# A graph attention kernel whose first 56 steps take one row in fourteen from rows of x that were gathered early

## The reference, cut to what matters

```
def _gat_layer(h_in, W, a_s, a_d, b, src, dst, n):
    h = (h_in @ W).reshape(n, Hh, Cc)
    alpha_s = jnp.sum(h * a_s, axis=-1)
    alpha_d = jnp.sum(h * a_d, axis=-1)
    e = jax.nn.leaky_relu(alpha_s[src] + alpha_d[dst], 0.2)
    m = jax.lax.stop_gradient(jax.ops.segment_max(e, dst, num_segments=n))
    ex = jnp.exp(e - m[dst])
    alpha = ex / jax.ops.segment_sum(ex, dst, num_segments=n)[dst]
    out = jax.ops.segment_sum(h[src] * alpha[:, :, None], dst, num_segments=n)
    return out.reshape(n, Hh * Cc) + b
...
h = jnp.maximum(_layernorm(x, axis=-1), 0.0)
h = gelu(_gat_layer(h, W0, ...))      # layer 0
h = gelu(_gat_layer(h, W1, ...))      # layer 1
x = x + h
```

## Time and profile before

| | |
|---|---|
| median of 3 executions | 4951.69 us (4951.07 to 4952.96) |
| span of the profiled execution, first to last instruction | 4186.7 us |
| median less span | 765.0 us |
| first gather of layer 0 | at 160.65 us |
| last gather of layer 0 | at 2132.16 us |
| first gather of layer 1 | at 2175.73 us |

### The profile page before, as it was taken

One profiled execution on the slowest core, in us unless ns is written; L12 is line 12 of the kernel. 1 busy time (PEld: TensorE's weight loads), 2 busy tenths in 40 slices (PEclk: granted clock), 3 DMA queues, 4 the chain that ended last, 5 costly groups with the idle time before them and its releaser, 6 DMA issues.

```text
span 4186.7 us, 56110 instructions
## 1 busy us (share of the span) xinstructions
PE 2764.1 (66%) x9786; PEld 1887.3 (45%) x9786; DVE 3644.9 (87%) x13061; ACT 2255.3 (54%) x7170; POOL 3044.4 (73%) x3215
## 2 busy tenths in 40 slices
PE   7566676666676666667655666666666666666666
PEld 6344444444444444444433444444444444444444
DVE  6588888888888888888868999999999999999998
ACT  5355555555555555555544555555555555555555
POOL 4477777777777777777747777777777777777774
PEclk9777878777777777877777777777777777777777
DMA  7555555555555555555535555555555555555553
GB/s 227 169 148 152 152 151 153 152 152 152 152 152 151 150 150 152 152 150 153 150 104 148 158 158 158 160 159 159 159 159 159 158 159 159 159 159 156 159 157 103
DMA packets 326665, 645.47 MB, mean 154 GB/s; under 512 B 97682, under 2 KB 195386, under 8 KB 326634
## 3 DMA queue, kind: packets, MB, share of 16 engines
q0 software_dynamic: 152224, 429.04, 38.2%
q1 hardware_dynamic: 128664, 172.56, 13.4%
q10 hardware_dynamic: 45746, 43.56, 3.0%
HBM read 597.18 MB, written 47.71 MB: 154 GB/s over the span
## 4 chain that ended last, share of the span: by engine, by line
POOL 54%; issue 22%; PE 13%; DMA 7%; DVE 3%; POOLq 0%; SPq 0%; ACT 0%; ACTq 0%; DVEq 0%
POOL rows_all L512 53%; PE bank L1129 10%; DMA rows_all<-table,edge 5%; DMA edges<-rows_all 2%; PE bank L1137 1%; PE bank L1151 1%; DVE rows_all L890 1%; PE bank L1116 0%; DVE ahead L901 0%; DVE value L895 0%; DVE onehot L910 0%; DVE behind L903 0%; DMA before_i<-in_dst_dram 0%; PE bank L1117 0%; PE bank L1122 0%
## 5 line engine op out<-in xcount | busy, mean ns | idle before, releaser
L512 POOL DMA_INDIRECT rows_all<-table,edge x3136 | 2990.4, 954 | 1008.5 <-issue 978.7
L1129 PE MATMUL bank<-rows_all,onehot 128*128 128x264 f32 x6272 | 1871.6, 457 | 20.7 <-DVE rows_all L890 11.0
L1129 PEld LDWEIGHTS bank<-rows_all,onehot 128*128 128x128 f32 x6272 | 1383.7, 228 | 458.3 <-DVE rows_all L890 186.2
L587 ACT ACTIVATE rows_all<-rows_all 128x64 f32<-128x64 f32 x3584 | 878.3, 336 | 3.7
L1111 PE MATMUL bank<-onehotT,logit_p 128*128 128x448 bf16 x896 | 279.3, 448 | 769.9 <-DVE logit_p L881 769.9
L890 DVE TENSOR_TENSOR rows_all<-rows_all,bank 128x768 f32<-128x768 f32 (+1 forms) x672 | 658.6, 1036 | 0.0
L1111 PEld LDWEIGHTS bank<-onehotT,logit_p 128*128 128x128 bf16 x896 | 79.9, 110 | 925.1 <-DVE logit_p L881 861.9
L1116 PE MATMUL bank<-ident,ahead 128*4 128x128 f32 x224 | 83.6, 373 | 581.6 <-DVE behind L903 581.0
L910 DVE TENSOR_TENSOR onehot<-bank,dloc 128x1792 f32<-128x1792 f32 x224 | 453.4, 2024 | 7.7
L599 ACT ACTIVATE share<-node_d 128x8 f32<-128x8 f32 x224 | 46.8, 209 | 742.7 <-DVE node_d L959 742.7
L611 ACT ACTIVATE bank<-fall 128x56 f32<-128x56 f32 x224 | 49.5, 221 | 579.8 <-DVE fall L987 579.8
(11 more groups left out here) (173 smaller groups left out, 3694.2 us busy)
## 6 DMA issues: line engine op xcount, KB each, us to landing
dst_b<-dst_row SPq DMA_DIRECT2D x224, 448.0 KB, 4.1
rows_all<-table,edge POOLq DMA_INDIRECT x3136
self_row<-table SPq DMA_DIRECT2D x224, 132.0 KB
table<-row ACTq DMA_DIRECT2D x113, 132.0 KB
x_row<-in_x_dram SPq DMA_DIRECT2D x112, 128.0 KB, 2.5
out_dram<-y_out ACTq DMA_DIRECT2D x112, 128.0 KB
table<-row ACTq DMA_DIRECT2D x24, 528.0 KB, 4.3
xg<-in_x_dram SPq DMA_DIRECT2D x24, 512.0 KB, 3.8
```

The lines of the kernel that those rows point to most:

```text
L512: nc.gpsimd.indirect_dma_start(out=G[u][:, j, :], out_offset=None, in_=table[L][0:N, :], in_offset=bass.IndirectOffsetOnAxis(ap=index[:, j ...
L587: last = nc.scalar.activation(G4[t.u][:, j, h, 0:C], G4[t.u][:, j, h, 0:C], ACT.Copy, scale=G4[t.u][:, j, h, C:C + 1])
L1129: last = nc.tensor.matmul(bank[3 + t.half][:, 0:ROW], onehot[t.half][:, j, :], G[t.u][:, j, :], start=(j == 0), stop=(j == SLOTS - 1))
```

## The change

For the first 56 chunks the rows of one slot (the last, number 13) are no longer gathered from `table[0]`. Instead the rows of x for that slot are gathered into SBUF during the dense stage: POOL issues two such gathers after each of the 28 stores of the edge lists. DVE computes their means and variances (14 chunks per set, four sets; the first two sets between groups of the dense stage, the last two after it). In the first 56 steps of layer 0, ACT normalises the 128 rows (`early_norm`), PE transposes them (`early_transpose`) and multiplies them by the first layer's weights (`early_rows`), with an ACT copy in between (`early_copy`), and ACT moves the product into slot 13 of the step's buffer (`early_move`). POOL issues 13 gathers in these steps instead of 14.

The index list for the early gathers comes from the source indices, whose load moves ahead on SP. To make room for `early_x` (56 tiles of 128 rows), many buffers now share their space: those of the dense stage with those of the steps. So SP, ACT and DVE get waits for the end of the dense stage and its stores. The loop of layer 0 is split in a head (14 rounds) and a rest.

```
+    EARLY = 56
+    AHEAD = EARLY // NB
+    HEAD_SETS = 4
+    IN_SET = EARLY // HEAD_SETS
...
+        early_T = bank[7][:, 0:KC * P]
+        early_row = bank[7][:, 0:ROW]
...
-        xg = [sb(f"xg{b}", [P, GROUP, D]) for b in range(XB)]
+        xg = [groups_or_hots[:, b * GROUP * D:(b + 1) * GROUP * D].rearrange("p (t c) -> p t c", t=GROUP) for b in range(XB)]
...
@@ pipeline
+                if L == 0:
+                    run(0, -ROLES, counts, skip=ROLES, head=True, coming=True)
                 for j in range(ROLES - 1):
-                    run(0, j + 1 - ROLES, counts, skip=ROLES - 1 - j)
-                with eng.Fori(0, rounds_) as r:
+                    run(0, j + 1 - ROLES, counts, skip=ROLES - 1 - j, head=L == 0, coming=L == 0)
+                if L == 0:
+                    with eng.Fori(0, AHEAD - 2) as r:
+                        counts = {}
+                        for j in range(NB):
+                            run(r, j, counts, head=True, coming=True)
+                    counts = {}
+                    for j in range(NB):
+                        run(AHEAD - 2, j, counts, head=True, coming=j < NB - 1)
+                with eng.Fori(AHEAD - 1 if L == 0 else 0, rounds_) as r:
@@ SP
+            sp.dma_start(src_c[0:96, :], src[0:96 * CH].rearrange("(c e) -> c e", e=CH)).then_inc(first_src_landed, 16)
...
-            sp.dma_start(src_c[0:96, :], src[0:96 * CH].rearrange("(c e) -> c e", e=CH)).then_inc(src_landed, 16)
...
+            for k in range(2):
+                sp.wait_ge(hnT_done[k], GROUPS * GROUP // 2 + 1 + 1)
@@ POOL
             for n in range(PIECES):
                 piece = slice(n * PIECE, (n + 1) * PIECE)
                 pool.dma_start(to[0:CHUNKS, piece], whole[0:CHUNKS, piece]).then_inc(edges_stored, 16)
-
+                for c in range(n * EARLY // PIECES, (n + 1) * EARLY // PIECES):
+                    nc.gpsimd.indirect_dma_start(
+                        out=early_x[:, c, :], out_offset=None, in_=x[0:N, :],
+                        in_offset=bass.IndirectOffsetOnAxis(ap=early_i[:, c:c + 1], axis=0)).then_inc(early_landed[c // IN_SET], 16)
                 pool.wait_ge(edges_stored, 16 * (n + 1))
...
-                        for j in range(SLOTS):
+                        for j in range(slots):
...
+                if L == 0:
+                    with nc.gpsimd.Fori(0, AHEAD) as r:
+                        gather_round(r, {}, SLOTS - 1)
+                with nc.gpsimd.Fori(AHEAD if L == 0 else 0, rounds_ + 1) as r:
+                    gather_round(r, {}, SLOTS)
@@ ACT
+            def early_norm(e):
+                chunk = act.value_load(steps_i[0:1, T_CHUNK, bass.ds(e.k, 1)], min_val=0, max_val=EARLY - 1)
+                act.wait_ge(s["earlyT_done"], e.done(1))
+                nc.scalar.activation(early_h, early_x[:, bass.ds(chunk, 1), :].rearrange("p o c -> p (o c)"), ACT.Relu,
+                                     bias=early_shift[:, bass.ds(chunk, 1)], scale=early_rstd[:, bass.ds(chunk, 1)]).then_inc(s["early_normed"], 1)
+
+            def early_copy(e):
+                act.wait_ge(s["earlyT_done"], e.done(0))
+                act.wait_ge(s["early_row_done"], e.done(1))
+                nc.scalar.activation(early_hT[:], early_T.rearrange("c (k n) -> c k n", n=P), ACT.Copy).then_inc(s["earlyT_copied"], 1)
+
+            def early_move(e):
+                act.wait_ge(s["early_row_done"], e.done(0))
+                act.wait_ge(s["sum_done"], e.done(4))
+                nc.scalar.activation(G[e.u][:, SLOTS - 1, :], early_row, ACT.Identity).then_inc(s["early_row_moved"], 1)
...
@@ DVE
+            def early_stats_of(c0, c1):
+                dve.wait_ge(early_landed[c0 // IN_SET], 16 * IN_SET)
+                n = c1 - c0
+                for j in range(n):
+                    last = nc.vector.bn_stats(early_stats[:, j, :], early_x[:, c0 + j, :])
+                link(last)
+                for j in range(n):
+                    last = nc.vector.bn_aggr(early_mv[:, c0 + j, :], early_stats[:, j, :])
+                return last
...
+            link(early_stats_of(0, 3))
             fill_fields()
...
+            link(early_stats_of(2 * IN_SET, 3 * IN_SET))
+            early_stats_of(3 * IN_SET, EARLY).then_inc(early_scaled, 1)
...
             def take_values(t):
-                dve.wait_ge(s["landed"][t.u], t.landed(16 * SLOTS))
+                if t.head:
+                    dve.wait_ge(s["landed"][t.u], t.landed(16 * (SLOTS - 1)))
+                    dve.wait_ge(s["early_row_moved"], t.done(0))
...
@@ PE
+            def early_transpose(e, stored_):
+                pe.wait_ge(s["early_normed"], e.done(0))
+                pe.wait_ge(s["early_row_moved"], e.done(1))
+                if stored_:
+                    pe.wait_ge(s["row_copied"], stored_.done(0))
...
+            def early_rows(e):
+                pe.wait_ge(s["earlyT_copied"], e.done(0))
...
+                    if known_ and known_.head:
+                        pe.wait_ge(s["early_row_moved"], known_.done(0))
                     next_rows(stored_)
...
+                if coming:
+                    early_transpose(coming, stored_)
+                    early_rows(coming)
                 if known_:
                     logits_to_edges(known_)
```

More of the change, by code:

```diff
@@ L294, in pipeline, with run @@
             for L in range(2):
-                def run(r, first, counts, n=ROLES, skip=0):
-                    body(*[None if j < skip or j >= n else Step(eng, L, r, rounds_, first + j, counts) for j in range(ROLES)])
+                def run(r, first, counts, n=ROLES, skip=0, head=False, coming=False):
+                    steps_of = [None if j < skip or j >= n else Step(eng, L, r, rounds_, first + j, counts, head) for j in range(ROLES)]
+                    body(*steps_of, Step(eng, L, r, rounds_, first + ROLES, counts, True) if coming else None)
                 counts = {}
+                if L == 0:
+                    run(0, -ROLES, counts, skip=ROLES, head=True, coming=True)
                 for j in range(ROLES - 1):
-                    run(0, j + 1 - ROLES, counts, skip=ROLES - 1 - j)
-                with eng.Fori(0, rounds_) as r:
+                    run(0, j + 1 - ROLES, counts, skip=ROLES - 1 - j, head=L == 0, coming=L == 0)
[8 more added lines that the diff above has]
+                with eng.Fori(AHEAD - 1 if L == 0 else 0, rounds_) as r:
                     counts = {}
@@ L804, in _ @@
             count_up()
+            early_indices()
             LIST = TURNS - 4
-            with nc.vector.Fori(0, LIST) as i:
+            for j in range(XB):
+                between(Group(0, j), Group(0, j + 1))
+                if j == 1:
+                    early_list()
+            with nc.vector.Fori(1, LIST) as i:
                 for j in range(XB):
@@ L1153, in next_rows, with pe_body @@
                     last.then_inc(s["row_done"], 1)
-            def pe_body(stored_, finished, weighed, landed, known_):
+            def early_transpose(e, stored_):
[3 more added lines that the diff above has]
+                    pe.wait_ge(s["row_copied"], stored_.done(0))
+                for j in range(KC):
+                    last = nc.tensor.transpose(early_T[:, j * P:(j + 1) * P], early_h[:, j * P:(j + 1) * P], ident[:])
+                last.then_inc(s["earlyT_done"], 1)
+            def early_rows(e):
+                pe.wait_ge(s["earlyT_copied"], e.done(0))
+                for j in range(KC):
+                    last = nc.tensor.matmul(early_row, early_hT[:, j, :], w_ext[:, 0, j, :], start=(j == 0), stop=(j == KC - 1))
+                last.then_inc(s["early_row_done"], 1)
+            def pe_body(stored_, finished, weighed, landed, known_, coming):
                 if stored_:
```

120 lines of the change are left out of this document (91 added, 29 removed).

## The result

The change takes 4997.16 us (median of 4, 4982.2 to 5022.18) against 4951.88 us (4951.07 to 4952.96) before. The ratio is 1.0097 with a 95% interval of 1.007 to 1.0125. The forecast was 4918 us; the change is 45 us slower instead of 34 us faster.

A forecast was written before the change was run, and what follows sets the result against it. POOL's gathers were taken to bound each step, with DVE 1.4 us behind. Start +27 us and head -61 us made -34; span 4152.7 us plus 765.0 us outside the instructions gave 4918 us, range 4893 to 4962.

The forecast's parts named there:

- DVE's second semaphore: In the steps, DVE was to get only a second semaphore in a wait it already had; no cost was counted.
- Layer 1 ... do not change: Layer 1 and the second half of layer 0 were to keep their time; no term was counted for them.
- The base: Profiled span 4186.7 us, steps of 17.6 us, taken as typical; the 765.0 us up to the median kept as outside instructions.
- DVE's margin of 1.4 us: In layer 0 DVE was put 1.4 us per step behind POOL, the most that a step could gain.
- 16.5 us per step: Expected length of a head step with 13 gathers, down from 17.6 us.
- the drain's 16.1 us: Where layer 0 drains, two successive DVE products start 16.1 us apart, taken as DVE's step without waits.
- Removed gathers: Layer 0's head: 56 gathers fewer on POOL, 1.1 us per step, 61 us gained; ends 70 and 34 us.
- Edge lists and source load: At the start: early gathers lengthen POOL's chain of stores by 25 us, moved source-index load adds 2 us; +27 us.
- Rival 1: At the start: stores finish only with the gathers behind them, periods 6.1 us, chain +72 us, total 4965 us; chance 0.15.
- The 3.9 us: Edge-list stores: short periods become 3.9 instead of 3.3 us if a store cannot land before the gather ahead of it.
- Products on ACT and PE: Head steps: added ACT and PE work mostly hidden in their waits for DVE; up to 1 us per step if cover is gone.
- Rival 2: Head: late copy on ACT or PE's sums push DVE, step settles at 17.0 us, gain 34 us, 4945 us; chance 0.20.

The follow-up runs named there:

- b1: The kernel before, unchanged, profiled again beside its timed executions: 4949.97 us, ratio 0.9998, steps 21.06 us apart.
- b3: The change's dense part alone (early gathers, statistics, shared buffers, split loop), 14 gathers per step, no products: 4974.64 us, 1.0043 of the kernel before.
- b4: The change without products in the head, 13 gathers there, slot 13 zero, dense part kept: 4891.1 us, 0.9882 of the kernel before.
- e4: The change without DVE's second wait behind the head and with `early_copy` behind the `Gelu`, full products: 4908.79 us, 0.9908 of the kernel before.
- d: Runs on one slower chip: the change without head products, 4980.57 us; with products, `early_copy` behind the `Gelu` and no second DVE wait behind the head, 5042.76 us.
- e1: The change without products, but ACT does its three head instructions on SBUF data and PE nothing: 4896.15 us, 0.9883 of the kernel before.
- e2: The change without products, but PE transposes and multiplies fixed operands in the head and ACT does nothing: 4886.64 us, 0.9875 of the kernel before.
- e3: The change with both ACT's and PE's head work but no wait between the two for it: 4903.29 us, 0.9910 of the kernel before.
- c1: The change without DVE's second wait behind the head, copy still ahead of the `Gelu`: 5044.12 us, 1.0017 of the kernel before.
- c3: The change without DVE's second wait behind the head and with `early_copy` behind the `Gelu`: 5032.0 us, 0.9987 of the kernel before.
- c4: The change, unchanged, measured again on a slower chip: 5114.15 us, 1.0126 of the kernel before.
- f1: The change, unchanged, measured once more on another slower chip: 5093.2 us, 1.012 of the kernel before.
- f2: The change without DVE's second wait behind the head, copy ahead of the `Gelu`, measured once more: 5057.45 us, 1.0036 of the kernel before.
- f: Side-by-side runs on one slower chip: the change, 5093.2 us, and the change without DVE's second wait behind the head, 5057.45 us.
- c: Four runs on one slower chip, among them the change, 5114.15 us, and the change without DVE's second wait behind the head, 5044.12 us.
- c2: The kernel before with one already met wait more per step on DVE: 5058.01 us, 1.0023 of the kernel before.
- d4: The kernel before with SP's load of `self_row` made once instead of per step: 5012.49 us, 0.9953 of the kernel before.
- b2: The kernel before with 13 gathers in all 224 steps, slot 13 zero: 4727.92 us, 0.955 of the kernel before.

## Why the prediction was wrong

Two steps of the prediction failed. The step that turned the sign is the term that it put at nothing: DVE's second semaphore, and with it "Layer 1 ... do not change". The other is its base, the profiled execution, which made all margins per step wrong but did not cost the gain.

In the profiled execution the change came out at +71.3 us where -34 were forecast, 105 us apart: layer 1 +84.5, the head +31 (-29.7 for -61), the start -9 (+18.3 for +27), the rest -2. Without layer 1's 84.5 us the change would have been 13 us shorter than the kernel before, even in this slowest of its executions.

**The base: that the profiled execution stands for the timed ones, and that the 765 us between span and median lie outside the instructions and stay.** All spans profiled later, of both kernels, end about 2 us below their own time. The 762 us are 3.4 us in each of 224 steps, in pauses as those of b1. So POOL's pace of 1.256 us per gather times 14 was not the whole step, and DVE's margin of 1.4 us, 16.5 us per step and the drain's 16.1 us described an execution that did not recur.

**Removed gathers: right in kind, sized too low.** Forecast 1.1 us per head step, -61 us. Measured without the products: 1.5 us per step (19.54 against 21.06), -83.5 us from b3 to b4.

**Edge lists and source load: close in sum, by luck in part.** The first gather came at 180.1 us, forecast 188: +19 for +27. Two terms were off in opposite directions. The stores' chain grew by 15.6 us, not 25, and the load of the source indices cost 4.5 us, not 2: the chain of waits of the change has it as

```profile
10.76 13.51 DMA before_i<-in_dst_dram
```

against the earlier trace rows. The stores stand 4.11 us apart (forecast 4.4), from 53.6 to 164.5 us. Waits for their landing, in one period of the middle and at the end, timeline of POOL:

```profile
80.87 0.58 POOL L529 DMA_DIRECT2D edges<-rows_all  x1 [2.08 <-DMA edges<-rows_all]
81.76 0.97 POOL L531 DMA_INDIRECT early_x<-in_x_dram,early_i  x1 [0.30 <-issue]
83.04 1.12 POOL L531 DMA_INDIRECT early_x<-in_x_dram,early_i  x1 [0.30 <-issue]
86.32 0.58 POOL L529 DMA_DIRECT2D edges<-rows_all  x1 [2.16 <-DMA edges<-rows_all]
...
161.44 0.58 POOL L529 DMA_DIRECT2D edges<-rows_all  x1
162.32 0.97 POOL L531 DMA_INDIRECT early_x<-in_x_dram,early_i  x1 [0.30 <-issue]
163.60 0.95 POOL L531 DMA_INDIRECT early_x<-in_x_dram,early_i  x1 [0.30 <-issue]
164.55 0.58 POOL L529 DMA_DIRECT2D edges<-rows_all  x1
```

Up to 149 us the periods lie between 3.1 and 6.4 us, 4.3 on average; the last six are 3.1 us, which is POOL's own work (3.32 in the prediction). Half of the stores wait for a landing at all, 25.6 us in 14 waits. (The row at 147.52 us in the earlier trace rows, which the prediction takes for the last of the 28 stores, is the first store behind them; the 28 periods are right.) Rival 1 wanted over 5.6 us on average; it did not happen, and the slower result is not its doing. The 3.9 us that the prediction worked out for the short periods from the Trainium skill's "DMA: Bandwidth & Descriptors" (section "Queues, rings and completion order") were not paid. That does not speak against the rule: the store at 161.44 had landed by 164.55, and the gather ahead of it, issued at 160.50, was due after the 3.77 us of the earlier trace rows at 164.3.

**Products on ACT and PE: put at nothing beyond the 16.5 us, and not free.** They cost 18 to 22 us on the chips that run the kernel before at 4950 us (e4) and 62 us on the chip of d. Each engine alone has room (e1, e2). The prediction followed the copy to ACT's `Gelu` and gave PE's wait of 3.64 us as cover, but it did not price the path of five handoffs in a row (normalise, transpose, copy, multiply, move), each behind other work in order. The profiled heads fit with that path as the cause (e4's is 24 us longer than b4's and 18 longer than e3's); the medians of e3 and e4 do not bear it out, so it stays an argument. Rival 2 named the effect; that its 34 us of gain lie near the 29.7 measured is chance, since it took them from a step of 17.0 us that did not exist. In the change itself the head is 25 us longer than in e4 (1150.7 against 1125.8), in profiled executions on two chips that run the kernel before alike; the copy ahead of the `Gelu` and the second wait are what differs. Whether either is the cause was not settled: c1 and c3 differ by 12 us, inside their spread, and the head of c4 is 30 us longer than that of c1, but the head of f1 is 25 us shorter than that of f2, with the same edit between them.

**"DVE gets nothing but a second semaphore in a wait that it has already" and "Layer 1 ... do not change": wrong, and the largest item.** The second semaphore is an instruction of its own in the loop, in all 224 steps: DVE's round has 274 instructions with it and 270 without. With it DVE's loop was fetched again in each round of layer 1: +84.5 us in the profiled execution, 36 to 70 us in the medians of f and c. The change with this wait alone taken out was measured on the slower chips only (1.0017 in c, 1.0036 in f). On a chip like that of the forecast e4, which also has the copy behind the `Gelu`, is at 0.9908, and 86 of the 108 us between its span and the change's are in layer 1 (2336.7 against 2422.6), where that copy is not made.

What stays open: why a stretch of slow sequencer instructions comes in nearly every step of a timed execution and not in the trace used for the prediction; why three chips run the kernel before 80 us slower than two others; what holds up the head when the products are added; and at which place of the loop in DVE's program the fetches begin.

## What to carry to other kernels

Compare the span of a profiled execution with the measured time before anything is worked out from it: where hundreds of microseconds are missing, the steps in the trace are not the steps that are timed. A wait that is always met is still an instruction; in a loop that is repeated a hundred times, look at the queue that brings instructions before and after. And price a chain across two engines by its own length as well as by the idle time of the engines it visits, and measure it with a kernel that has the work without the handoffs, over enough executions to tell their medians apart.

## What the runs showed of the hardware that was not expected

- In the change, one wait more or less in DVE's loop decides between 130 and 3 instruction packets (8 KB each) in layer 1, and between a stall of 4.0 us per round and none. In the kernel before a loop of the same 274 instructions (c2) brings neither.
- In timed executions SP's register instructions take 0.70 us each through some 7 to 8 us of nearly every step (217 of 221 in b1; 201 in the change, 188 in e4), and DVE instructions with nothing but met waits are late by up to 2.7 us (`mean_o` in b1). It stays without the load of `self_row` (d4) and with one gather less (b2).
- A gather left out is worth more than its issue time in layer 0 (1.55 us against 1.25) and less than half of it in layer 1 (0.50 us), both in b2.
